# Prologue of a fused attention and mixture-of-experts kernel: the weights loaded on ScalarE's DMA queue beside x, and the order of the first image's statistics, the fold and the memsets rewritten

## The chip, the cores and the metric

The kernel runs as one program on one core of one Trainium2 chip. The metric is the device time in microseconds of that core, the median of several executions. A trace of one profiled execution gives the rows shown below; its engines are TensorE (PE, its weight loads PEld), VectorE (DVE), ScalarE (ACT), GpSimd (POOL) and SyncE (SP). SP, ACT and POOL can also issue DMAs, each on a queue of its own (q1 is SP's, q10 is ACT's, q0 is GpSimd's); all the queues use the same 16 DMA engines.

## The reference, cut to what is computed

```python
# x: (4, 256, 64, 64) float32
x = x + conv_attn(group_norm(x), Wq, bq, Wk, bk, Wv, bv, Wo, bo)
#   conv_attn: instance norm, then for each pixel softmax over its 3x3 neighbours of (q . k) / 16,
#   the weighted sum of v, times Wo, plus bo
t = to_tokens(x)                                     # (4, 4096, 256)
t = t + windowed_gate(layer_norm(t), Wp, bp, Wg)     # sums over a window of 64 tokens
t = t + moe(layer_norm(t), router_w, w1, b1, w2, b2) # 8 experts, top 2
x = from_tokens(t)
```

group_norm and the instance norm need the mean and the variance of all 4096 pixels of an image for each channel, so no pixel of an image can be normalized before all of that image has been read.

## The kernel before, in words

The order of the work is written out by hand. Each engine has its own instruction stream, with explicit semaphores. `enter` and `leave` make a barrier between parts: a part starts when all five engines have left the one before. The parts are a prologue, a token loop (attention, gate, routing) over 32 blocks of 8 image rows (512 tokens, 8 blocks for each of 4 images), a loop over expert tiles, and an output loop. The change touches the prologue and the first lines of the token loop.

The prologue does these things:

- **Weights.** 12 DMAs: the four 256x256 matrices `wq_s`, `wk_s`, `wv_s`, `wo_s` (256 KB each, moved as 256 rows of 1 KB), `wp_s` and `rw_s`, the four biases `bq_s` to `bo_s` (256 single elements of 4 bytes each), `bp_s` and `wg_s`. All raise the semaphore `w_in`, and PE, ACT and DVE all wait for the twelve together (`w_in` at 16 * 12).
- **x of the first image.** Eight DMAs of 512 KB (256 rows of 2 KB each) into the ring `xs` of XR = 8 slots, one semaphore `x_seen` for each slot; then `load_rows(0)`, the first block again with its halo rows into `raw` (3 DMAs). As slots come free (`x_done`), four blocks of the second image follow (EARLY = 4), and then `load_rows(1)` and `load_rows(2)`.
- **Statistics on DVE.** Two `bn_stats` a block (L531) for 12 blocks; after the eighth, `block_means` (L303, L306) aggregates the first image. Then come the group sums: PE multiplies by a block-diagonal matrix (`group_product`, L310), DVE subtracts and squares (`group_spread`, L316 to L320), PE multiplies again, `group_variance` (L325), POOL takes a power of -0.5 (`group_root`, L330), `channel_variance` (L334 to L338), a second power, and `image_scales` (L342, L344).
- **The fold.** PE multiplies Wq by Wk and Wv by Wo, with the bias products (L477, 44 matmuls), ACT copies the results out of PSUM (L499 to L504) and rounds them into the high halves of `wqk2` and `wvo2` (L507), and POOL subtracts to get the low halves (L464), which raises `folded` to 3.
- DVE waits for `folded` at 3, adds `q_const` into `edge` (L541) and raises `prepared`, for which every engine waits on entering the token loop. There DVE's memsets and small copies (L1213 to L1221) raise `cleared` to 5, for which PE, ACT and POOL wait.

The first block of the token loop is normalized by ACT (`normed`, L1024) and POOL (L1578), rounded by ACT (`band`, L1034), and split by DVE (`band_lower`, L1390). PE's first matmul (L758) waits for that. DVE's stream has the statistics of a block of the second image (`x_seen_blocks`, L1411) before `band_lower`; that block, in `xs1`, is loaded by SP as the first thing after `prepared`.

Of the kernel before, what the change touches and what calls it, by code (L numbers as in the profile page):

```python
# [88 lines left out]
def hybrid(nc, x, wqT, wkT, wvT, wo, bq, bk, bv, bo, wpT, bp, wg, rwT, w1, b1, w2, b2, out):  # L89
# [6 lines left out]
    ACT = mybir.ActivationFunctionType  # L96
    AX = mybir.AxisListType

    P = 128
# [29 lines left out]
    with ctx:  # L129
# [118 lines left out]
        def pb(name, shape, dt=f32):  # L248
            return prep.enter_context(nc.sbuf_tensor(name, shape, dt))
# [14 lines left out]
        bo_s = pb("bo_s", [P, CC, 1])  # L264
        bqb = pb("bqb", [P, CC, P])
        XR = 8
        xs = pb("xs", [P, XR, CC, BT])

        w_in = sem("w_in")
        x_in = [sem(f"x_in{i}") for i in range(XROWS)]  # L270
        w_experts = sem("w_experts")
# [83 lines left out]
        def prologue_sync(eng):  # L355
            for dst, src in ((wq_s, wqT), (wk_s, wkT), (wv_s, wvT), (wo_s, wo), (wp_s, wpT), (rw_s, rwT)):
                eng.dma_start(dst[:, :, :], src.rearrange("(c p) n -> p c n", p=P)).then_inc(w_in, 16)
            for dst, src in ((bq_s, bq), (bk_s, bk), (bv_s, bv), (bo_s, bo)):
                eng.dma_start(dst[:, :, :], src.unsqueeze(2)).then_inc(w_in, 16)
            eng.dma_start(bp_s[:, :], bp).then_inc(w_in, 16)  # L360
            eng.dma_start(wg_s[:, :], wg).then_inc(w_in, 16)

            for i in range(XR):
                eng.dma_start(xs[:, i, :, :], xv[:, :, i // IB, i % IB * BT:(i % IB + 1) * BT])\
                   .then_inc(x_seen[i], 16)
            load_rows(eng, 0)
            for i in range(EARLY):
                eng.wait_ge(x_done[i], 1)
                eng.dma_start(xs[:, i, :, :], xv[:, :, 1, i * BT:(i + 1) * BT]).then_inc(x_seen[i], 16)
            for blk in range(1, XROWS):  # L370
                load_rows(eng, blk)
            leave(eng, 0)

        def prologue_gpsimd(eng):
# [85 lines left out]
            eng.wait_ge(pool_const, done)  # L460

            eng.wait_ge(folded, 2)
            for two, whole in ((wqk2, wqk), (wvo2, wvo)):
                last = eng.tensor_tensor(two[:, 1, :, :], whole[:, :, :], two[:, 0, :, :].bitcast(f32),  # L464
                                         ALU.subtract)
            last.then_inc(folded, 1)
            for n in range(2):
                group_root(eng, 0, n)
            leave(eng, 0)

        def prologue_tensor(eng):
            eng.wait_ge(w_in, 16 * 12)
            eng.wait_ge(dve_const, 1)

            def product(bank, cols, lhs, rhs):
                for d in range(CC):
                    last = eng.matmul(bank[:, cols], lhs(d), rhs(d), start=(d == 0), stop=(d == CC - 1))  # L477
                return last
            for c in range(CC):
                cs = slice(c * P, c * P + P)  # L480
                product(m_bank[c], slice(0, C), lambda d: wq_s[:, d, cs], lambda d: wk_s[:, d, :])
                product(m_bank[c], slice(C, C + 1), lambda d: wk_s[:, d, cs], lambda d: bq_s[:, d, :])
                product(m_bank[c], slice(C + 1, C + 2), lambda d: wq_s[:, d, cs], lambda d: bk_s[:, d, :])
                product(m_bank[2 + c], slice(0, C), lambda d: wv_s[:, d, cs], lambda d: wo_s[:, d, :])
                product(m_bank[2 + c], slice(C, C + 1), lambda d: wo_s[:, d, cs], lambda d: bv_s[:, d, :])
            product(s_bank[0], slice(0, 1), lambda d: bqb[:, d, :], lambda d: bk_s[:, d, :]).then_inc(fold, 1)

            eng.wait_ge(pool_const, 23)
            for n in range(2):
                group_product(eng, 0, n, s_bank[1]).then_inc(g_sum, 1)  # L490
            leave(eng, 0)

        def prologue_scalar(eng):
            eng.wait_ge(w_in, 16 * 12)
            eng.wait_ge(kept, 1)
            eng.wait_ge(fold, 1)

            for c in range(CC):
                eng.activation(wqk[:, c, :], m_bank[c][:, 0:C], ACT.Copy, scale=-SCALE)  # L499
                eng.activation(r_bias[:, c, :], m_bank[c][:, C:C + 1], ACT.Copy, scale=-SCALE)  # L500
                eng.activation(wvo[:, c, C:C + 1], m_bank[c][:, C + 1:C + 2], ACT.Copy, scale=-SCALE)
                eng.activation(wvo[:, c, 0:C], m_bank[2 + c][:, 0:C], ACT.Copy)
                eng.activation(o_bias[:, c, :], m_bank[2 + c][:, C:C + 1], ACT.Identity, bias=bo_s[:, c, :])
            eng.activation(q_const[:, :], s_bank[0][:, 0:1], ACT.Copy, scale=-SCALE).then_inc(folded, 1)  # L504
            eng.wait_ge(folded, 1)
            for two, whole in ((wqk2, wqk), (wvo2, wvo)):
                last = eng.activation(two[:, 0, :, :], whole[:, :, :], ACT.Copy)  # L507
            last.then_inc(folded, 1)
            leave(eng, 0)

        def prologue_vector(eng):
            for c in range(CC):
                last = eng.memset(wvo[:, c, C + 1:C + 2], 0.0)
            last.then_inc(kept, 1)
            eng.wait_ge(w_in, 16 * 12)
            eng.tensor_copy(bqb[:, :, :], bq_s[:, :, :].broadcast_to([P, CC, P])).then_inc(dve_const, 1)

            eng.wait_ge(pool_const, 23)
# [7 lines left out]
            eng.tensor_scalar(base[:, 0, :], base0[:, 0, :], float(CAP), None, ALU.mult)  # L526

            for i in range(XR + EARLY):
                eng.wait_ge(x_seen[i % XR], i // XR * 16 + 16)
                for c in range(CC):  # L530
                    last = eng.bn_stats(stats[:, c, i, :], xs[:, i % XR, c, :])  # L531
                last.then_inc(x_done[i % XR], 1)
                if i == XR - 1:
                    eng.wait_ge(x_done[i], 1)
                    block_means(eng, 0)
            group_spread(eng, 0, s_bank[1])
            group_variance(eng, 0, s_bank[1])
            channel_variance(eng, 0)
            image_scales(eng, 0)
            eng.wait_ge(folded, 3)  # L540
# [198 lines left out]
        def token_loop_tensor(eng):  # L739
            enter(eng, 0)  # L740
            eng.wait_ge(prepared, 1)
            eng.wait_ge(cleared, 5)

# [211 lines left out]
        def token_loop_scalar(eng):  # L955
            enter(eng, 0)
            eng.wait_ge(prepared, 1)
            eng.wait_ge(cleared, 5)

# [250 lines left out]
        def token_loop_vector(eng):  # L1210
            enter(eng, 0)
            eng.wait_ge(prepared, 1)
            eng.memset(xn1[:, :, :], 0.0).then_inc(cleared, 1)  # L1213
            eng.memset(tail_id[:, :, :, :], 0.0).then_inc(zeroed, 1)
            eng.memset(blank[:, :, :], 0.0).then_inc(zeroed, 1)
            eng.wait_ge(cleared, 1)
# [3 lines left out]
            eng.memset(xn1[:, :, C:C + 1], 1.0).then_inc(cleared, 1)  # L1220
            eng.memset(besti[:, :, :].rearrange(flat), 0).then_inc(cleared, 1)  # L1221

# [298 lines left out]
        def token_loop_gpsimd(eng):  # L1521
            enter(eng, 0)
            eng.wait_ge(prepared, 1)
            eng.wait_ge(cleared, 5)
            eng.iota(jvec[:, :], pattern=[[1, NJ]], base=0, channel_multiplier=0,
# [506 lines left out]
```

## Time and profile before

| what | value |
|---|---|
| median of 3 runs | 1447.72 us (1446.48 to 1451.52) |
| profiled execution, its own time | 1442.31 us |
| its span in the trace | 1440.5 us |
| busy share of the span: PE, PEld, DVE, ACT, POOL | 89%, 78%, 78%, 69%, 52% |
| first 40.4 us: until PE's first matmul of the token loop | 2.8% of the span |

The busy shares are means over parts with different limits. The profiled execution lies 5.4 us below the median of the others, so a difference worked out on the trace is to be added to the median and not compared with it directly.

### The profile page before, as it was taken

To read this page: it belongs to the slowest core of one execution; us is meant where nothing else is said; L and a number is where in the kernel's file an instruction comes from. 1 tells how busy PE (TensorE), PEld (TensorE's weight loads), DVE (VectorE), ACT (ScalarE), POOL (GpSimd) and SP (SyncE) were. 2 spreads that over 40 slices of the span, in tenths; PEclk is the share of its full clock that TensorE was granted. 3 is DMA by queue.
4 is the path that set the end of the run, shared out by engine and by line. 5 is a ranking of instruction groups with operands and counts; after the bars stand their busy time and mean duration, and the time that the engine had idled before them with its cause. 6 is when DMAs were issued, how large, how long until landed. Compare 5 with 4: busy or idle time off the path is not lost. (4 is left out here: it accounts for less than half of the span.)

```text
span 1440.5 us, 28874 instructions
## 1 busy us (share of the span) xinstructions
PE 1285.4 (89%) x8512; PEld 1130.3 (78%) x8512; DVE 1127.6 (78%) x3903; ACT 987.1 (69%) x2090; POOL 746.9 (52%) x963
## 2 busy tenths in 40 slices
PE   3799999999999999999999589999999999993434
PEld 3688888888888888888887478899999999982334
DVE  5478888888888777878786778899999999983323
ACT  1677777777777777777775468888888888871223
POOL 2115656566656566566655465566566656662000
PEclk9999999999999999999999679999999999996555
DMA  8622535363542122222111189988888888856999
GB/s 273 216 83 80 149 86 148 88 156 89 147 117 91 58 83 64 82 69 86 50 42 57 36 277 326 300 270 270 277 271 270 273 263 275 279 194 273 416 400 350
DMA packets 148216, 264.00 MB, mean 183 GB/s; under 512 B 52576, under 2 KB 74720, under 8 KB 143840
## 3 DMA queue, kind: packets, MB, share of 16 engines
q1 hardware_dynamic: 113440, 173.78, 38.6%
q0 software_dynamic: 25920, 71.60, 14.0%
q10 hardware_dynamic: 8704, 16.78, 3.0%
q8 instruction: 73, 1.20, 0.4%
q14 instruction: 79, 0.65, 0.2%
HBM read 128.39 MB, written 100.68 MB: 159 GB/s over the span
## 5 line engine op out<-in xcount | busy, mean ns | idle before, releaser
L1716 POOL DMA_INDIRECT answers<-yy,dest_i x284 | 276.7, 974 | 176.7 <-DVE yy L1837 99.7
L1558 POOL DMA_INDIRECT sent<-tn,slot_s x256 | 275.5, 1076 | 146.7 <-issue 79.2
L1768 PE MATMUL s_bank<-band,hh 128*128 x568 | 163.2, 287 | 0.6 <-DVE yy L1872 0.6
L1768 PE MATMUL s_bank<-w_s,hh 128*128 x568 | 157.2, 277 | 0.0
L1768 PE MATMUL s_bank<-band,hl 128*128 x568 | 157.0, 276 | 0.0
L1802 ACT ACTIVATE hid<-m_bank,b1s 128x512 f32<-128x512 f32 x142 | 97.7, 688 | 78.3 <-PE m_bank L1751 50.3
L1822 ACT ACTIVATE zz<-xin 128x256 f32<-128x256 f32 x284 | 147.5, 602 | 0.0
L758 PE MATMUL m_bank<-wvo,band 128*128 128x258 f32 x792 | 132.7, 304 | 13.3 <-DVE band L1390 10.9
L1535 POOL TENSOR_TENSOR rs<-ve,halves 128x4 f32<-128x4 f32 x64 | 64.9, 1019 | 153.7 <-DVE ve L1252 153.7
L790 PE MATMUL o_bank<-vv,at 128*128 128x256 f32 x512 | 138.7, 393 | 1.3 <-DVE tt L1300 0.8
L758 PEld LDWEIGHTS m_bank<-wvo,band 128*128 128x128 f32 x792 | 107.1, 192 | 29.4 <-issue 27.7
L1938 PE MATMUL m_bank<-ident,tot 128*128 128x128 f32 x256 | 54.6, 391 | 80.7 <-ACT fin L1952 58.6
L1837 DVE SCALAR_TENSOR_TENSOR yy<-yy,pick,zz 128x256 f32<-128x256 f32 x284 | 118.7, 480 | 7.4
L758 PE MATMUL s_bank<-band,rT 128*128 128x256 f32 x768 | 123.1, 296 | 0.0
L1751 PE MATMUL m_bank<-xh,w1hs 128*128 128x512 f32 x284 | 112.5, 396 | 4.5 <-DMA b2s<-in_b 4.5
L1938 PEld LDWEIGHTS m_bank<-ident,tot 128*128 128x128 f32 x256 | 46.1, 207 | 89.1 <-issue 66.6
L1751 PE MATMUL m_bank<-xh,w1ls 128*128 128x512 f32 x284 | 112.4, 396 | 0.0
L1751 PE MATMUL m_bank<-xl,w1hs 128*128 128x512 f32 x284 | 112.1, 395 | 0.0
L1926 DVE TENSOR_TENSOR tot<-got 128x1024 f32<-128x1024 f32 x32 | 39.1, 1225 | 92.6 <-PE m_bank L1938 64.9
L1952 ACT ACTIVATE fin<-m_bank 128x512 f32<-128x512 f32 x64 | 34.9, 595 | 107.6 <-DMA out_x<-fin 77.1
L1768 PEld LDWEIGHTS s_bank<-band,hh 128*128 128x128 f32 x568 | 106.8, 188 | 0.9 <-issue 0.8
L1768 PEld LDWEIGHTS s_bank<-w_s,hh 128*128 128x128 f32 x568 | 106.9, 188 | 0.1
(238 smaller groups left out, 3658.9 us busy)
## 6 DMA issues: line engine op xcount, KB each, us to landing
xin<-sent SPq DMA_DIRECT2D x71, 524.0 KB, 4.7
got<-answers SPq DMA_DIRECT2D x32, 1024.0 KB, 9.7
w1hs<-rT SPq DMA_DIRECT2D x71, 256.0 KB
w1ls<-w_s SPq DMA_DIRECT2D x71, 256.0 KB
xs<-in_x SPq DMA_DIRECT2D x32, 512.0 KB, 5.0
raw<-in_x SPq DMA_DIRECT2D x32, 512.0 KB
out_x<-fin ACTq DMA_DIRECT2D x32, 512.0 KB, 10.0
b2s<-in_b SPq DMA_DIRECT2D x71, 128.0 KB
```

The lines of the kernel that those rows point to most:

```text
L758: last = eng.matmul(dst, lhs(i, c), rhs(j, c), start=(n == 0), stop=(n == len(passes) - 1))
L790: last = eng.matmul(o_bank[:, 0:C], at[:, k % 2, j, :], vv[:, value_slot(it.block("B"), k + j), 0:C], start=(j == 0), stop=(j == 1))
L1535: eng.tensor_tensor(rs[:, n, :], ve[:, n, :], halves[:, 0, 0:KT], ALU.pow).then_inc(root.sem, 1)
L1558: eng.indirect_dma_start(sent, bass.IndirectOffsetOnAxis(slot_s[:, par, j, k:k + 1], 0), tn[:, par, k, :], None).then_inc(scattered[par], 16)
L1716: eng.indirect_dma_start(answers, bass.IndirectOffsetOnAxis(dest_i[:, at_ % RING, k:k + 1], 0), yy[:, slot, k, :], None).then_inc(rows_out ...
L1751: last = eng.matmul(h_bank[f][:, :], w[:, at_ % WS, c, fs], xx[:, par, c, :], start=(n == 0), stop=(n == 3 * CC - 1))
L1768: last = eng.matmul(y_bank[half][:, k * C:(k + 1) * C], hx[:, par, f, ts], rhs, start=(n == 0), stop=(n == 3 * CC - 1))
L1802: eng.activation(hid[:, f, :], h_bank[f][:, :], ACT.Gelu, bias=b1s[:, at_ % WS, f:f + 1])\
L1822: last = eng.activation(zz[:, at_ % WS, k, :], row[:, 0:C], ACT.Identity, bias=row[:, C + 5:C + 6], scale=row[:, C + 4:C + 5])
L1837: last = eng.scalar_tensor_tensor(row, row, pick[:, at_ % RING, k:k + 1], zz[:, at_ % WS, k, :], ALU.mult, ALU.add)
L1926: eng.tensor_tensor(tot[:, it.parity("K"), :, :], got[:, blk % GOT, :, 0, :], got[:, blk % GOT, :, 1, :], ALU.add).then_inc(tot_ready.sem, 1)
L1938: last = eng.transpose(turned_bank(it, c)[:, k * P:(k + 1) * P], tot[:, it.parity("K"), k, c * P:(c + 1) * P], ident[:, :])
```

## The change

The twelve weight DMAs move from SP's queue to ACT's, each matrix followed by its bias; SP starts with x. The eight DMAs that the fold needs raise a semaphore of their own, `w_fold`; the other four raise `w_in`, for which only PE waits, ahead of the group sums. ACT runs a one-element activation (`warm`) ahead of the fold and takes the fold's results in two halves. DVE does three memsets at the head, moves its constants (L519 to L526) behind the first image's `block_means`, and does the scales of the first image in between the blocks of the second. POOL does the two `group_root` before the fold's subtractions. In the token loop a memset of 1032 columns shrinks to 4.

```diff
@@ prologue_sync
-            for dst, src in ((wq_s, wqT), (wk_s, wkT), (wv_s, wvT), (wo_s, wo), (wp_s, wpT), (rw_s, rwT)):
-                eng.dma_start(dst[:, :, :], src.rearrange("(c p) n -> p c n", p=P)).then_inc(w_in, 16)
-            for dst, src in ((bq_s, bq), (bk_s, bk), (bv_s, bv), (bo_s, bo)):
-                eng.dma_start(dst[:, :, :], src.unsqueeze(2)).then_inc(w_in, 16)
-            eng.dma_start(bp_s[:, :], bp).then_inc(w_in, 16)
-            eng.dma_start(wg_s[:, :], wg).then_inc(w_in, 16)
-
             for i in range(XR):
                 eng.dma_start(xs[:, i, :, :], xv[:, :, i // IB, i % IB * BT:(i % IB + 1) * BT])\
                    .then_inc(x_seen[i], 16)
@@ prologue_gpsimd
+            for n in range(2):
+                group_root(eng, 0, n)
             eng.wait_ge(folded, 2)
             for two, whole in ((wqk2, wqk), (wvo2, wvo)):
                 last = eng.tensor_tensor(two[:, 1, :, :], whole[:, :, :], two[:, 0, :, :].bitcast(f32),
                                          ALU.subtract)
             last.then_inc(folded, 1)
-            for n in range(2):
-                group_root(eng, 0, n)
@@ prologue_tensor
-            eng.wait_ge(w_in, 16 * 12)
+            eng.wait_ge(w_fold, 16 * 8)
             eng.wait_ge(dve_const, 1)
...
-                product(m_bank[2 + c], slice(C, C + 1), lambda d: wo_s[:, d, cs], lambda d: bv_s[:, d, :])
+                product(m_bank[2 + c], slice(C, C + 1), lambda d: wo_s[:, d, cs], lambda d: bv_s[:, d, :]).then_inc(fold, 1)
...
             eng.wait_ge(pool_const, 23)
+            eng.wait_ge(w_in, 16 * 4)
@@ prologue_scalar
-            eng.wait_ge(w_in, 16 * 12)
+            def matrix(dst, src, landed):
+                eng.dma_start(dst[:, :, :], src.rearrange("(c p) n -> p c n", p=P)).then_inc(landed, 16)
+
+            for (dst, src), (bias, given) in (((wq_s, wqT), (bq_s, bq)), ((wk_s, wkT), (bk_s, bk)), ((wv_s, wvT), (bv_s, bv)),
+                                              ((wo_s, wo), (bo_s, bo))):
+                matrix(dst, src, w_fold)
+                eng.dma_start(bias[:, :, :], given.unsqueeze(2)).then_inc(w_fold, 16)
+            matrix(rw_s, rwT, w_in)
+            matrix(wp_s, wpT, w_in)
+            eng.dma_start(bp_s[:, :], bp).then_inc(w_in, 16)
+            eng.dma_start(wg_s[:, :], wg).then_inc(w_in, 16)
             eng.wait_ge(kept, 1)
-            eng.wait_ge(fold, 1)
+            eng.activation(warm[:, :], wvo[:, 0, C + 1:C + 2], ACT.Copy)
+            eng.wait_ge(w_fold, 16 * 8)
 
             for c in range(CC):
+                eng.wait_ge(fold, c + 1)
...
+            eng.wait_ge(fold, CC + 1)
@@ prologue_vector
-            eng.wait_ge(w_in, 16 * 12)
+            eng.memset(tail_id[:, :, :, :], 0.0).then_inc(zeroed, 1)
+            eng.memset(blank[:, :, :], 0.0).then_inc(zeroed, 1)
+            eng.memset(besti[:, :, :].rearrange(flat), 0).then_inc(zeroed, 1)
+            eng.wait_ge(w_fold, 16 * 8)
             eng.tensor_copy(bqb[:, :, :], bq_s[:, :, :].broadcast_to([P, CC, P])).then_inc(dve_const, 1)
+
+            def seen(i, c):
+                if c == 0:
+                    eng.wait_ge(x_seen[i % XR], i // XR * 16 + 16)
+                last = eng.bn_stats(stats[:, c, i, :], xs[:, i % XR, c, :])
+                if c == CC - 1:
+                    last.then_inc(x_done[i % XR], 1)
+
+            for i in range(XR):
+                for c in range(CC):
+                    seen(i, c)
+            eng.wait_ge(x_done[XR - 1], 1)
+            block_means(eng, 0)
 
             eng.wait_ge(pool_const, 23)
...
+            group_spread(eng, 0, s_bank[1])
+            seen(XR, 0)
+            group_variance(eng, 0, s_bank[1])
+            seen(XR, 1)
+            channel_variance(eng, 0)
+            seen(XR + 1, 0)
+            image_scales(eng, 0)
+            seen(XR + 1, 1)
+            for i in range(XR + 2, XR + EARLY):
                 for c in range(CC):
-                    last = eng.bn_stats(stats[:, c, i, :], xs[:, i % XR, c, :])
-                last.then_inc(x_done[i % XR], 1)
...
@@ token_loop_vector
-            eng.memset(xn1[:, :, :], 0.0).then_inc(cleared, 1)
-            eng.memset(tail_id[:, :, :, :], 0.0).then_inc(zeroed, 1)
-            eng.memset(blank[:, :, :], 0.0).then_inc(zeroed, 1)
+            eng.memset(xn1[:, :, C + 1:C + 2], 0.0).then_inc(cleared, 1)
...
-            eng.memset(besti[:, :, :].rearrange(flat), 0).then_inc(cleared, 1)
```

**The weights' DMAs.** On SP, at the start of the program, the weights stood ahead of x before (three more matrices like the first row stand above these rows, and `in_...` is the tensor in HBM):

```order
L357 DMA wo_s<-in_wo 128x2x256
L357 DMA wp_s<-in_wpT 128x2x128
L357 DMA rw_s<-in_rwT 128x2x8
L359 DMA bq_s<-in_bq 128x2
L359 DMA bk_s<-in_bk 128x2
L359 DMA bv_s<-in_bv 128x2
L359 DMA bo_s<-in_bo 128x2
L360 DMA bp_s<-in_bp 128x1
L361 DMA wg_s<-in_wg 128x1
L364 DMA xs<-in_x 128x2x512 x8
```

On ACT, the start of the changed program:

```order
L491 DMA wq_s<-in_wqT 128x2x256
L496 DMA bq_s<-in_bq 128x2
L491 DMA wk_s<-in_wkT 128x2x256
L496 DMA bk_s<-in_bk 128x2
L491 DMA wv_s<-in_wvT 128x2x256
L496 DMA bv_s<-in_bv 128x2
L491 DMA wo_s<-in_wo 128x2x256
L496 DMA bo_s<-in_bo 128x2
L491 DMA rw_s<-in_rwT 128x2x8
L491 DMA wp_s<-in_wpT 128x2x128
L499 DMA bp_s<-in_bp 128x1
L502 ACT_TABLE_LOAD
```

All twelve left SP, where the eight DMAs of x now stand first; on ACT each bias stands behind its matrix.

**The first image's scales.** On DVE before, from the end of `block_means` to the end of the prologue (`g` stands for g1, g2 and g3):

```order
L306 COPY g<-mv 128x2
L531 BN_STATS stats<-xs 128x6 x8
L316 TENSOR_TENSOR g<-g,s_bank 128x2
L318 TENSOR_TENSOR g<-g 128x2
L320 TENSOR_TENSOR g<-g,mv 128x2
L325 TENSOR_SCALAR g<-s_bank 128x2
L334 TENSOR_TENSOR g<-g 128x2
L336 TENSOR_TENSOR g<-g,mv 128x2
L338 TENSOR_SCALAR g<-g 128x2
L342 TENSOR_TENSOR s_all<-g 128x2
L344 SCALAR_TENSOR_TENSOR b_all<-g,s_all 128x2
L541 TENSOR_SCALAR edge<-edge,q_const 128x1
```

On DVE in the changed program, from the second instruction of `group_spread` on:

```order
L320 TENSOR_TENSOR g<-g 128x2
L322 TENSOR_TENSOR g<-g,mv 128x2
L533 BN_STATS stats<-xs 128x6
L327 TENSOR_SCALAR g<-s_bank 128x2
L533 BN_STATS stats<-xs 128x6
L336 TENSOR_TENSOR g<-g 128x2
L338 TENSOR_TENSOR g<-g,mv 128x2
L340 TENSOR_SCALAR g<-g 128x2
L533 BN_STATS stats<-xs 128x6
L344 TENSOR_TENSOR s_all<-g 128x2
L346 SCALAR_TENSOR_TENSOR b_all<-g,s_all 128x2
L533 BN_STATS stats<-xs 128x6 x5
```

The eight `bn_stats` of the second image stood ahead of the chain; now three stand inside it and five behind it.

**The powers and the fold on POOL.** Before, at the end of the prologue and the start of the token loop:

```order
L464 TENSOR_TENSOR wqk<-wqk 128x512
L464 TENSOR_TENSOR wvo<-wvo 128x516
L330 TENSOR_TENSOR g<-g,halves 128x2 x2
L1525 IOTA jvec 128x71
L1529 IOTA tail_id 128x60
```

The same place in the changed program:

```order
L332 TENSOR_TENSOR g<-g,halves 128x2 x2
L461 TENSOR_TENSOR wqk<-wqk 128x512
L461 TENSOR_TENSOR wvo<-wvo 128x516
L1545 IOTA jvec 128x71
L1549 IOTA tail_id 128x60
```

The two powers moved ahead of the two subtractions.

## Rows read from the trace of the kernel before

**Rows 1.** The page: busy tenths of PE in 40 slices.

```profile
PE   3799999999999999999999589999999999993434
```

**Rows 2.** Timeline of SP's issues: start, us, engine, line.

```profile
0.80 0.45 SPq L357 DMA_DIRECT2D wq_s<-in_wqT  x1
...
6.26 0.43 SPq L361 DMA_DIRECT2D wg_s<-in_wg  x1
...
33.39 5.78 SPq L707 DMA_DIRECT2D xs<-in_x  x3
```

**Rows 3.** Timeline, the fold on PE and DVE beside it.

```profile
8.33 0.29 DVE L516 COPY bqb<-bq_s 128x256 f32<-128x256 f32 x1 [7.37 <-DMA wg_s<-in_wg]
...
8.77 2.04 PE L477 MATMUL m_bank<-wk_s,wq_s 128*128 128x256 f32 x4 [8.77 <-DVE bqb L516]
...
13.91 8.05 DVE L531 BATCH_NORM_STATS2 stats<-xs 128x6 f32<-128x512 f32 x12 [0.67 <-DMA xs<-in_x]
...
20.71 0.99 PE L477 MATMUL s_bank<-bk_s,bqb 128*128 128x1 f32 x4
```

**Rows 4.** Timeline, the first image's scales.

```profile
22.63 0.17 DVE L306 COPY g<-mv 128x2 f32<-128x2 f32 x1
...
29.27 0.14 DVE L316 TENSOR_TENSOR g<-g,s_bank 128x2 f32<-128x2 f32 x1
...
29.86 0.59 PE L310 MATMUL s_bank<-g,group 128*128 128x2 f32 x2 [6.36 <-DVE g L320]
30.49 0.16 DVE L325 TENSOR_SCALAR g<-s_bank 128x2 f32<-128x2 f32 x1 [0.68 <-PE s_bank L310]
...
31.48 0.16 DVE L334 TENSOR_TENSOR g<-g 128x2 f32<-128x2 f32 x1 [0.84 <-POOL g L330]
...
32.12 0.70 POOL L330 TENSOR_TENSOR g<-g,halves 128x2 f32<-128x2 f32 x1 [0.67 <-DVE g L338]
...
33.13 0.27 DVE L541 TENSOR_SCALAR edge<-edge,q_const 128x1 f32<-128x1 f32 x1
```

**Rows 5.** Timeline, the fold's copies on ACT and POOL.

```profile
21.81 1.28 ACT L499 ACT_TABLE_LOAD   x1 [21.81 <-PE s_bank L477]
...
25.50 0.62 ACT L507 ACTIVATE wvo<-wvo 128x516 fp32r<-128x516 f32 x1
26.26 1.26 POOL L464 TENSOR_TENSOR wqk<-wqk 128x512 fp32r<-128x512 f32 x1 [17.34 <-ACT wvo L507]
```

**Rows 6.** Timeline, the start of the token loop.

```profile
33.78 0.92 DVE L1213 MEMSET xn<- 128x1032 f32 x1 [0.39 <-DVEq L350]
...
35.78 1.52 ACT L1024 ACTIVATE normed<-raw,b_all,s_all 128x512 f32<-128x512 f32 x2 [9.67 <-issue]
...
37.33 1.27 ACT L1034 ACTIVATE band<-normed 128x1280 fp32r<-128x1280 f32 x1
37.49 1.29 DVE L1411 BATCH_NORM_STATS2 stats<-xs 128x6 f32<-128x512 f32 x2 [1.88 <-DMA xs<-in_x]
...
38.70 1.54 DVE L1390 TENSOR_TENSOR band<-normed,band 128x640 fp32r<-128x640 f32 x2
...
40.39 1.63 PE L758 MATMUL m_bank<-wvo,band 128*128 128x258 f32 x6 [9.94 <-DVE band L1390]
```

**Rows 7.** Windows: length, busy of each engine, PEclk, DMA share, GB/s last.

```profile
0.00:2.00 2.00, 0.00 (x0) 0.00 (x0) 0.09 (x2) 0.00 (x0) 1.11 (x10) 1.00 0.06 5
2.00:4.00 2.00, 0.00 (x0) 0.00 (x0) 0.00 (x0) 0.00 (x0) 1.50 (x7) 1.00 0.94 292
...
10.00:15.00 5.00, 5.00 (x19) 4.46 (x19) 3.67 (x6) 0.00 (x0) 0.00 (x0) 1.00 1.04 394
```

**Rows 8.** DMA queues, 6 to 8 us: packets, MB, share of 16 engines.

```profile
q1 hardware_dynamic: 887, 0.09, 41.0%
```

**Rows 9.** DMA queues, 1370 to 1376 us, in the output loop.

```profile
q1 hardware_dynamic: 275, 1.99, 79.8%
q10 hardware_dynamic: 280, 0.54, 23.2%
```

More of the change, by code:

```diff
@@ L265, in hybrid @@
         bqb = pb("bqb", [P, CC, P])
+        warm = pb("warm", [P, 1])
         XR = 8
@@ L269, in hybrid @@
         w_in = sem("w_in")
+        w_fold = sem("w_fold")
         x_in = [sem(f"x_in{i}") for i in range(XROWS)]
@@ L526, in prologue_vector @@
             eng.tensor_scalar(base[:, 0, :], base0[:, 0, :], float(CAP), None, ALU.mult)
-            for i in range(XR + EARLY):
-                eng.wait_ge(x_seen[i % XR], i // XR * 16 + 16)
-                for c in range(CC):
-                    last = eng.bn_stats(stats[:, c, i, :], xs[:, i % XR, c, :])
-                last.then_inc(x_done[i % XR], 1)
[L533 to L539, printed above, removed]
+            group_spread(eng, 0, s_bank[1])
[7 more added lines that the diff above has]
+            for i in range(XR + 2, XR + EARLY):
+                for c in range(CC):
+                    seen(i, c)
             eng.wait_ge(folded, 3)
@@ L741, in token_loop_tensor @@
             eng.wait_ge(prepared, 1)
-            eng.wait_ge(cleared, 5)
+            eng.wait_ge(cleared, 4)
             def begin(it, job):
@@ L957, in token_loop_scalar @@
             eng.wait_ge(prepared, 1)
-            eng.wait_ge(cleared, 5)
+            eng.wait_ge(cleared, 4)
             def take(it, job, out_, in_=None, func=ACT.Copy, **k):
@@ L1523, in token_loop_gpsimd @@
             eng.wait_ge(prepared, 1)
-            eng.wait_ge(cleared, 5)
+            eng.wait_ge(cleared, 4)
             eng.iota(jvec[:, :], pattern=[[1, NJ]], base=0, channel_multiplier=0,
```

## The prediction

> **What bounds the kernel now.** I read the page's slices first. PE is at nine tenths or more from the third slice to the 36th, except in two slices in the middle, where one part gives way to the next [rows 1]. So what stands ahead of the token loop is a serial head: a microsecond more or less in it should reach the end nearly whole, since no part behind it runs to a clock of its own. The change works only in that head, which is why the rest of the trace matters little here.
>
> The timeline of the first 41 us gives the head as three stretches. Call W the moment when DVE sees the weights.
>
> - Until W = 8.33, PE and DVE do nothing of note: the last weight, issued at 6.26, is what both wait for [rows 2, 3].
> - From W on, PE folds until 21.70 (20.71 + 0.99), which is W + 13.4, while DVE takes statistics as fast as x lands [rows 3]. The chain of the scales then ends with `edge` at 33.13, and SP issues the first load of the token loop at 33.39: `prepared` is at W + 25.1 [rows 2, 4].
> - From 33.39 to PE's first matmul at 40.39 it is 7.0 us [rows 2, 6].
>
> What matters in this reading is that both engines hang on W, and that the chain from `group_spread` (29.27) to 33.13 waits for nothing but DVE's queue: the group sum was due long before, `mv` being copied at 22.63, but the blocks of the second image stand in front [rows 4].
>
> **The part after W, which gets shorter.** In the changed order DVE goes from W into 16 statistics at 0.671 each (8.05 / 12) [rows 3], 10.7 us, and has the means about 0.9 later, at W + 12.0. Seven constants follow, each a copy of the size of `bqb` (0.29) or smaller, so at most 2.0 us in the 2.1 until the group sum is there. PE is the later one: it ends the fold at W + 13.4, does the group product, and its result reaches DVE 0.63 later, as from 29.86 to 30.49 [rows 4]: `group_spread` starts at W + 14.1. The chain itself took 3.86 us (29.27 to 33.13) [rows 4]. The three statistics put inside it lie in its waits (about 29.8 to 30.49, 30.65 to 31.48, 32.1 to 32.82): 0.67 fits each time but for 0.05 us. Five remain behind it, 3.36 us, and 0.26 from `edge` to SP's issue. Sum: 14.1 + 3.86 + 0.05 + 3.36 + 0.26 = W + 21.6. That is 3.4 us less than W + 25.1.
>
> POOL's swap costs nothing: ACT ends its rounding at about W + 15 now that the 1.28 us table load is ahead of the fold and half of the copies lie beside PE (before: 26.12) [rows 5]. The powers end at W + 17.6, and the two subtractions of 2.5 us follow (1.26 and as much again, [rows 5]), so `folded` is 3 at W + 20.2, 1.2 us before DVE asks. Without that cover each microsecond would count. The table load and the halves are hidden likewise. The three early memsets lie before W.
>
> The shorter memset of the token loop looks like 0.9 us off the path (33.78 to 34.70), and with the moved ones I estimate 1.4 of the 2.0 us until ACT starts at 35.78 [rows 6]. I cost it at nothing. DVE's statistics of the block in `xs1` stand in front of `band_lower`, and they wait until 37.49 for a load that SP issued at 33.39; they end at 38.78, after ACT's `band` at 38.60 [rows 2, 6]. With ACT 1.4 us earlier the load still decides: 4.1 + 1.3 + 1.6 = 7.0 us from `prepared` to PE, as before. The bound from the other side is 1.4 us gained.
>
> **W itself, which gets later.** Before, the weights had the DMA engines to themselves. Now x is on SP's queue from the same moment. The trace of before has no two queues competing in the prologue, but the output loop has: SP loads 8 KB packets, ACT stores 2 KB packets, both with more queued than is moved. From 1370 to 1376 us the queues moved 275 and 280 packets, 1.99 and 0.54 MB [rows 9]. The turn goes one packet to each queue, whatever its size.
>
> Now count packets. The fold needs 4 x 256 rows of 1 KB and 4 x 256 single elements of a bias: 2048 packets. Against each stands one row of x of 2 KB, and SP has 8 x 256 = 2048 of these queued, and `raw` behind them, before it waits for anything. The small biases, 4 KB in all, are the costly half: each element lets a 2 KB row of x pass. So the eight weight DMAs land when all eight blocks of x have gone too:
>
> - x, 4.19 MB at 394 GB/s [rows 7]: 10.6 us;
> - matrices, 1.05 MB at 292 GB/s [rows 7]: 3.6 us;
> - biases: 887 mostly small packets took 41% of 2 us [rows 8], 14.8 ns of one engine each, so 1024 of them over 16 engines 0.95 us.
>
> 15.2 us, from the first packet at 2.0 (the share is 0.06 before, 0.94 after) [rows 7], and some 0.8 from the last packet to the wait that sees it: of the 2.07 from the last weight's issue at 6.26 to 8.33, 1.2 is what the first issue at 0.80 took to its first packet [rows 2, 3, 7]. An estimate: W = 18.0 instead of 8.33.
>
> The bounds: with equal bytes for both queues W would be 10.7 (below); with the weights first, 7.3; with small packets or pairs dearer than alone, 21. I take 18.0, because the six microseconds of [rows 9] are two queues of this core, both backlogged, and nothing in them favours either.
>
> DVE cannot use x while it waits: `bqb` stands ahead of the statistics and needs `w_fold`. That is the second half of the cost, for x's first block will lie there from about 5.5 us (2.0, 16 pairs of packets on each engine, and the landing).
>
> **Sum.** `prepared` moves from 33.4 to 18.0 + 21.6 = 39.6: +6.2 us. PE's first matmul of the loop comes at 46.6. On the profiled execution that is 1442.3 + 6.2 = 1448.5, on the median 1447.7 + 6.2 = 1453.9. What a measurement of this kernel can tell from no change is 0.3%, 4.3 us; W = 11.8 would be no change, above 16.1 it can be told.
>
> The Trainium skill speaks against this edit too. "DMA: Bandwidth & Descriptors", section "Issuing engines are not separate DMA queues", says that issuing from several engines saves only the sequencer's time and that the transfers interleave on the same 16 engines. The trace agrees: both queues share one stretch in [rows 9].
>
> **Rivals.**
>
> *Larger turns.* If several small packets went in one turn, up to 4 KB, four rows of weights would face two of x, and a bias's 16 elements on an engine one turn. Then 40 rows of x pass on each engine, 1.31 MB or 3.3 us, and W = 2.0 + 3.3 + 3.6 + 0.95 + 0.8 = 10.7. `prepared` is at 32.3: -1.1 us, 1446.6. For it speaks that the packets of [rows 9] are too large and too few in size to show a grouping of 4-byte ones; against it, that 2 KB packets went one by one there and not two by two. The same page of the Trainium skill, section "SWDGE vs HWDGE vs iDMA", describes for GpSimd's path a packet of preferably up to 4096 bytes as the unit after which an engine turns to another queue; no row of before shows that for ACT's.
>
> *The weights win, and it ends faster.* If ACT's queue is served ahead of x, for instance since SP's descriptors for 2 KB rows come slower than the engines ask, the fold's data take 2.0 + 3.6 + 0.95 + 0.8: W = 7.3. `prepared` at 28.9, -4.5 us, 1443.2; the point from which this is faster by over 0.3% is W = 7.5. Four of the twelve DMAs no longer count for the wait, which speaks for some gain; equal turns in [rows 9] against it.
>
> *The delay does not reach the end.* W is late as forecast, but part of the 6.2 us is given back, say 3 or more, as the clock granted to PE or the meeting of transfers in the loops changes. 1450 or so. PE's dense slices [rows 1] speak against it.
>
> **How the numbers follow.** One packet a turn, W between 16 and 21, time 1452 to 1457: 0.58. Larger turns: 0.23. Weights first: 0.09. Delay given back: 0.10. Over 4.3 us slower is most of the first, 0.51; faster is the third with a little of the second, 0.12; the rest within. The range leaves out a tenth on each side: from 1444.5, where the faster cases begin, to 1458.5, W = 21 with a microsecond or so of spread. The likeliest case alone is 1451.5 to 1457.5.
>
> **What would show it.** In the trace after: DVE's `bqb` at about 18 (the whole forecast hangs on it); equal counts of packets on q1 and q10 from 2 to 17 us; PE's fold 13.4 long from there; statistics without a wait for x, 16 in a row; `group_spread` at W + 14; `folded` before DVE asks; `prepared` at W + 21.6; from there 7.0 to PE, with the wait for `xs1` still in front of `band_lower`. It is wrong if `bqb` comes before 12, or if PE's first loop matmul moves and the end does not.

## The result and the profile after

The changed kernel takes 1452.19 us (median of 20 runs, 1447.24 to 1457.92), the kernel before in the same sets 1448.75 us (20 runs, 1442.49 to 1453.54). The ratio is 1.0025, 95% interval 1.0013 to 1.0037: 3.4 us slower by the medians, 3.6 by the ratio (0.0025 of 1449). That is a loss, since the interval does not reach 1 (it stands for 1.9 to 5.4 us), and it is smaller than the 4.3 us that the prediction set as what can be told. 1453.9 was forecast. Ratios here and below leave out runs over 1.5% above the fastest of the same kernel, while medians take in all runs.

The timeline of the changed kernel, rows that answer to [rows 2 to 6] (start, us, engine, line, operation):

```profile
0.81 4.71 SPq L359 DMA_DIRECT2D xs<-in_x  x8
0.81 0.49 ACTq L491 DMA_DIRECT2D wq_s<-in_wqT  x1
...
5.05 0.55 ACTq L496 DMA_DIRECT2D bo_s<-in_bo  x1
...
15.46 0.29 DVE L528 COPY bqb<-bq_s 128x256 f32<-128x256 f32 x1 [13.78 <-DMA bo_s<-in_bo]
15.67 9.58 DVE L533 BATCH_NORM_STATS2 stats<-xs 128x6 f32<-128x512 f32 x16
...
15.90 2.05 PE L472 MATMUL m_bank<-wk_s,wq_s 128*128 128x256 f32 x4 [15.90 <-DVE bqb L528]
...
27.84 0.99 PE L472 MATMUL s_bank<-bk_s,bqb 128*128 128x1 f32 x4
...
29.29 0.16 DVE L318 TENSOR_TENSOR g<-g,s_bank 128x2 f32<-128x2 f32 x1 [2.45 <-PE s_bank L312]
...
32.90 1.26 POOL L461 TENSOR_TENSOR wqk<-wqk 128x512 fp32r<-128x512 f32 x1
32.96 1.21 DVE L344 TENSOR_TENSOR s_all<-g 128x2 f32<-128x2 f32 x1 [0.21 <-POOL g L332]
34.12 1.27 POOL L461 TENSOR_TENSOR wvo<-wvo 128x516 fp32r<-128x516 f32 x1
34.21 1.20 DVE L346 SCALAR_TENSOR_TENSOR b_all<-g,s_all 128x2 f32<-128x2 f32 x1
35.33 3.05 DVE L533 BATCH_NORM_STATS2 stats<-xs 128x6 f32<-128x512 f32 x5
35.59 5.47 SPq L730 DMA_DIRECT2D xs<-in_x  x3
38.30 0.25 DVE L564 TENSOR_SCALAR edge<-edge,q_const 128x1 f32<-128x1 f32 x1
...
39.15 1.52 ACT L1047 ACTIVATE normed<-raw,b_all,s_all 128x512 f32<-128x512 f32 x2 [8.93 <-issue]
...
39.38 1.29 DVE L1431 BATCH_NORM_STATS2 stats<-xs 128x6 f32<-128x512 f32 x2 [0.40 <-DMA xs<-in_x]
...
42.00 1.56 DVE L1410 TENSOR_TENSOR band<-normed,band 128x640 fp32r<-128x640 f32 x2 [1.33 <-ACT band L1057]
...
43.71 1.63 PE L781 MATMUL m_bank<-wvo,band 128*128 128x258 f32 x6 [13.23 <-DVE band L1410]
```

Read it from the fold's weights. The last of them, a bias of 1 KB, was issued at 5.05 and landed 10.4 us later: `bqb` comes at 15.46 instead of 8.33 [rows 3], so W is 7.1 us late. From there the way to the loop is shorter than before: DVE's 16 statistics run without a wait (9.58 us), the group sum is used at W + 13.8 instead of 20.9 [rows 4], and PE's first loop matmul stands at W + 28.25 instead of W + 32.06 [rows 3, 6]. 7.13 lost and 3.81 won give 43.71 instead of 40.39: +3.32 us. The end moved by 3.4 to 3.6 us, which agrees within the interval.

The DMA queues of the changed kernel from 3 to 15 us (packets, MB, share of 16 engines; q1 carries x, q10 the weights):

```profile
q1 hardware_dynamic: 1733, 3.35, 76.7%
q10 hardware_dynamic: 1681, 1.03, 28.8%
```

As many packets of the one as of the other, though x moved three times the bytes.

### The profile page after: what moved, and what is told of

The parts are those of the page before. It is cut to its first block and busy times, and to the rows that moved or that the text cites. A ratio compares the mean times of both kernels' runs of the same rounds, so it can differ in the third digit from the quotient of the medians.

```text
span 1454.7 us, 28875 instructions
## 1 busy us (share of the span) xinstructions
PE 1291.1 (89%) x8512; PEld 1131.6 (78%) x8512; DVE 1128.3 (78%) x3903; ACT 988.1 (68%) x2091; POOL 752.1 (52%) x963
## 5 line engine op out<-in xcount | busy, mean ns | idle before, releaser
L1736 POOL DMA_INDIRECT answers<-yy,dest_i x284 | 279.7, 985 | 174.4 <-DVE yy L1857 100.5
L813 PE MATMUL o_bank<-vv,at 128*128 128x256 f32 x512 | 143.9, 405 | 1.4 <-DVE tt L1320 0.8
```

Source lines behind the costliest of these rows:

```text
L813: last = eng.matmul(o_bank[:, 0:C], at[:, k % 2, j, :], vv[:, value_slot(it.block("B"), k + j), 0:C], start=(j == 0), stop=(j == 1))
L1736: eng.indirect_dma_start(answers, bass.IndirectOffsetOnAxis(dest_i[:, at_ % RING, k:k + 1], 0), yy[:, slot, k, :], None).then_inc(rows_out ...
```

## The experiments

The kernels were timed in three sets, on three chips. In the first set the kernel before took 1448.7 us, in the other two 1561.9 and 1609.8 (medians); ratios and differences of the device time are always within a set. The head of the program differs little between them: with the weights' DMAs as changed and unsplit, the fold's weights were there between 15.46 and 16.12 us in all three. So positions in the timelines are compared across sets, best as distances from W. The kernel before was traced in the first set alone.

### The weights back on SP, ahead of x

```diff
@@ prologue_sync
+            for (dst, src), (bias, given) in (((wq_s, wqT), (bq_s, bq)), ((wk_s, wkT), (bk_s, bk)), ((wv_s, wvT), (bv_s, bv)),
+                                              ((wo_s, wo), (bo_s, bo))):
+                matrix(dst, src, w_fold)
+                eng.dma_start(bias[:, :, :], given.unsqueeze(2)).then_inc(w_fold, 16)
...
             for i in range(XR):
@@ prologue_scalar
-            for (dst, src), (bias, given) in (((wq_s, wqT), (bq_s, bq)), ((wk_s, wkT), (bk_s, bk)), ((wv_s, wvT), (bv_s, bv)),
-                                              ((wo_s, wo), (bo_s, bo))):
...
```

The four DMAs that raise `w_in` move along.

Expected:

> The changed kernel with its twelve weight DMAs back on SP's queue ahead of x, all else as changed. Theory (the head decides, and the weights' landing is what got late): bqb comes at about 7 us instead of 15.5 (1.05 MB at 292 GB/s, 512 small packets, 2.0 ahead and 0.8 behind), the statistics are again as fast as x lands, and PE's first matmul of the token loop comes at about 38 us: 2.4 us ahead of the kernel before, 5.7 ahead of the change. Device time about 1446.5 where before is 1448.8. Rival (the other edits, or the loops, carry the loss): it stays at or above the kernel before.

Measured: 1445.74 us (12 runs) beside 1448.68, ratio 0.9991 (0.9972 to 1.0009). The timeline:

```profile
7.50 0.56 DVE L528 COPY bqb<-bq_s 128x256 f32<-128x256 f32 x1 [5.82 <-DMA bo_s<-in_bo]
...
10.60 10.78 DVE L533 BATCH_NORM_STATS2 stats<-xs 128x6 f32<-128x512 f32 x16 [2.54 <-DMA xs<-in_x]
...
37.39 1.63 PE L781 MATMUL m_bank<-wvo,band 128*128 128x258 f32 x6 [13.23 <-DVE band L1410]
```

PE starts the loop 6.3 us ahead of the change and 3.0 ahead of before, and DVE now waits for x instead of for the weights. The place of the weights is the loss: nothing else was edited, and this ratio's interval lies wholly below the change's (1.0013 to 1.0037). Whether this kernel is faster than the one before the interval leaves open (2.9 us by the medians, 1.3 by the ratio).

### Only the queue

```diff
@@ prologue_sync
-            for dst, src in ((wq_s, wqT), (wk_s, wkT), (wv_s, wvT), (wo_s, wo), (wp_s, wpT), (rw_s, rwT)):
-                eng.dma_start(dst[:, :, :], src.rearrange("(c p) n -> p c n", p=P)).then_inc(w_in, 16)
...
@@ prologue_scalar
+            for dst, src in ((wq_s, wqT), (wk_s, wkT), (wv_s, wvT), (wo_s, wo), (wp_s, wpT), (rw_s, rwT)):
+                eng.dma_start(dst[:, :, :], src.rearrange("(c p) n -> p c n", p=P)).then_inc(w_in, 16)
...
```

This is an edit of the kernel before: all twelve DMAs in their old order, each still raising `w_in`.

Expected:

> The kernel before with its twelve weight DMAs moved to ACT's queue in their old order, and nothing else. Theory: all twelve land at about 20 us, beside x; from there 22.2 us to SP's first load of the loop and 7.0 to PE: first loop matmul at about 49.4 us instead of 40.4, device time about 9 us over before (0.6%). The other edits of the change must then be worth some 5.5 us. Rival (the queue costs nothing, the order on DVE does): within 1.5 us of before.

Measured: 1460.55 us (6 runs) beside 1448.68, ratio 1.0090 (1.0061 to 1.0118).

```profile
20.02 0.29 DVE L515 COPY bqb<-bq_s 128x256 f32<-128x256 f32 x1 [19.06 <-DMA wg_s<-in_wg]
...
41.16 0.16 DVE L334 TENSOR_TENSOR g<-g 128x2 f32<-128x2 f32 x1 [3.72 <-POOL g L330]
...
50.03 1.63 PE L757 MATMUL m_bank<-wvo,band 128*128 128x258 f32 x6 [12.78 <-DVE band L1389]
```

The queue alone costs 9.6 us in the head (50.03 - 40.39), inside the interval of 8.8 to 17.1 us at the end, though nearer to its lower bound than its centre of 13.0. The other edits, taken together, are thus worth 6.3 us of it (9.6 - 3.3), and 4.6 of these are W itself (20.02 against 15.46): eight DMAs to wait for instead of twelve, and another order.

The second row shows what POOL's swap takes away. With the subtractions still ahead of the powers, DVE waits 3.72 us for the first power, since POOL is at the subtractions from 37.96 to 40.4. In the kernel before they had been over by 28.8, ahead of the chain.

### The same bytes in twice the packets

```diff
@@ prologue_scalar, matrix()
-                eng.dma_start(dst[:, :, :], src.rearrange("(c p) n -> p c n", p=P)).then_inc(landed, 16)
+                for h in range(halves_of):
+                    cols = slice(h * C // 2, (h + 1) * C // 2) if halves_of == 2 else slice(None)
+                    eng.dma_start(dst[:, :, cols], src[:, cols].rearrange("(c p) n -> p c n", p=P)).then_inc(landed, 16)
```

Expected:

> The changed kernel with each of the four matrices moved as two DMAs of half rows: the same bytes, 2048 packets of 512 B instead of 1024 of 1 KB. Theory (one packet a turn): 2560 packets must go instead of 1536, and as many of SP's go with them, so bqb moves from 15.5 to about 19.6 us and PE's first loop matmul by about 4 us. Rival (bytes or larger turns decide): bqb stays within 0.7 us of 15.5.

`halves_of` is 2 for the four matrices of the fold. Measured: one time, 1454.30 us. The timeline, and the DMA queues from 3 to 19 us:

```profile
20.50 0.29 DVE L531 COPY bqb<-bq_s 128x256 f32<-128x256 f32 x1 [18.82 <-DMA bo_s<-in_bo]
...
26.90 1.85 PE L472 MATMUL m_bank<-wk_s,wq_s 128*128 128x256 f32 x4
...
29.40 1.11 PE L472 MATMUL m_bank<-wo_s,wv_s 128*128 128x256 f32 x4
...
46.21 1.63 PE L784 MATMUL m_bank<-wvo,band 128*128 128x258 f32 x6 [13.23 <-DVE band L1413]
```

```profile
q1 hardware_dynamic: 2809, 4.63, 81.3%
q10 hardware_dynamic: 2911, 1.06, 26.6%
```

W moved by 5.0 us (4.1 expected, 0 by bytes): it is the count of packets. The counts are near equal again. The 0.9 us beyond the expectation is not explained; from 19 to 20.5 us SP's queue was nearly empty (84 packets against 639), so the last of the weights no longer met x. PE's first loop matmul moved by only 2.5 us, which the theory did not have: four matmuls of the fold took 2.04 to 2.06 us up to 26.9, 1.85 in the group that begins there, and 1.11 from 29.4 on. The expectation's 4 us for it is a miss.

### Matmuls on PE while it waits

```diff
@@ prologue_tensor
+            eng.wait_ge(pool_const, 5)
+            for n in range(56):
+                eng.matmul(s_bank[1][:, 256:384], ones[:, :], ones[:, :], start=True, stop=True)
             eng.wait_ge(w_fold, 16 * 8)
```

Expected:

> The changed kernel with 56 matmuls of 128x128 ones on PE while it waits for the weights (their result is not used). Theory (the fold's matmuls run at half their later speed because PE comes from idling: in the run with half rows their duration fell from 0.51 to 0.28 us midway): the fold takes about 7 us instead of 12.9, the group sum waits for DVE instead, group_spread starts at about 26.9 instead of 29.3, and PE's first loop matmul comes 2.4 us earlier, at about 41.3. Rival (the speed belongs to something else, DMA traffic for one): the fold takes 12.9.

Measured: one time, 1549.37 us, in the set where before took 1561.92 (one run, from which no difference is read).

```profile
1.90 15.56 PE L469 MATMUL s_bank<-ones 128*128 128x128 f32 x112 [1.90 <-POOL ones L383]
15.79 0.29 DVE L531 COPY bqb<-bq_s 128x256 f32<-128x256 f32 x1 [14.12 <-DMA bo_s<-in_bo]
...
17.29 1.03 PE L475 MATMUL m_bank<-wk_s,wq_s 128*128 128x256 f32 x4
...
23.34 0.58 PE L475 MATMUL s_bank<-bk_s,bqb 128*128 128x1 f32 x4
...
41.58 1.63 PE L784 MATMUL m_bank<-wvo,band 128*128 128x258 f32 x6 [13.22 <-DVE band L1413]
```

Each of the 56 stands as two rows in the trace. The fold takes 6.6 us (17.29 to 23.92) instead of 12.9, though it starts 1.5 us behind W, when the 56 are through, and PE comes to the loop at W + 25.8, 2.5 us sooner. So the fold ran at half this speed in the kernel before and in the changed one. In none of the eleven traces without these matmuls did it start at the higher speed. In two it reached it midway (the one with half rows and the second run of the change), in nine never, and what decides between these the runs do not show. DMA traffic does not: the two stretches shown at the end of this document had 352 and 346 GB/s.

### POOL's subtractions behind the scales

```diff
@@ prologue_gpsimd
             for n in range(2):
                 group_root(eng, 0, n)
+            eng.wait_ge(scaled_images, 1)
             eng.wait_ge(folded, 2)
```

Expected:

> The changed kernel with one more wait: POOL starts the fold's two subtractions only when image_scales is done. Theory (DVE's two small operations of image_scales took 1.21 and 1.20 us instead of 0.16 because POOL's subtractions ran beside them): they take 0.16 to 0.17 again, the last statistics end 2.1 us earlier, folded is at 3 about 0.6 us later, and PE's first loop matmul comes at about 42.8 us instead of 43.7. Rival (they were slow for the value they waited for, not for POOL): they stay at 1.2 us. The device time can't tell it.

Measured: one time, 1444.27 us.

```profile
15.90 0.29 DVE L529 COPY bqb<-bq_s 128x256 f32<-128x256 f32 x1 [14.22 <-DMA bo_s<-in_bo]
...
33.40 0.16 DVE L344 TENSOR_TENSOR s_all<-g 128x2 f32<-128x2 f32 x1 [0.22 <-POOL g L332]
33.59 0.17 DVE L346 SCALAR_TENSOR_TENSOR b_all<-g,s_all 128x2 f32<-128x2 f32 x1
...
43.20 1.63 PE L782 MATMUL m_bank<-wvo,band 128*128 128x258 f32 x6 [12.28 <-DVE band L1411]
```

The two operations are back at 0.16 and 0.17 us, so it was POOL's instruction beside each that held them for its whole length. PE's first loop matmul stands at W + 27.3, 0.95 us sooner. The rest of the 2.1 us is lost at the load of `xs1`, for which DVE waits 2.98 us in this run: SP issues it at 36.53, W + 20.6 instead of W + 20.1, since `folded` comes later.

### The statistics not behind the weights

```diff
@@ prologue_vector
-            eng.wait_ge(w_fold, 16 * 8)
-            eng.tensor_copy(bqb[:, :, :], bq_s[:, :, :].broadcast_to([P, CC, P])).then_inc(dve_const, 1)
...
-            for i in range(XR):
+            for i in range(XR + EARLY):
+                if i == 6:
+                    eng.wait_ge(w_fold, 16 * 8)
+                    eng.tensor_copy(bqb[:, :, :], bq_s[:, :, :].broadcast_to([P, CC, P])).then_inc(dve_const, 1)
                 for c in range(CC):
                     seen(i, c)
+                if i == XR - 1:
+                    eng.wait_ge(x_done[XR - 1], 1)
+                    block_means(eng, 0)
...
             group_spread(eng, 0, s_bank[1])
-            seen(XR, 0)
             group_variance(eng, 0, s_bank[1])
-            seen(XR, 1)
...
```

PE waits for `dve_const` only ahead of its last product, and no `seen` is left between the steps of the scales.

Expected:

> The changed kernel with DVE's statistics no longer behind the weights: bqb is copied ahead of the seventh block, PE waits for it only before its last product, and all twelve blocks stand ahead of the scales. The DMAs stay as changed. Theory (DVE's wait for the fold's weights costs only what it leaves behind the group sum, PE's fold is the later one): the group sum still starts at about 29 us, but no statistics stand behind the scales, which POOL's subtractions again draw out to about 35.4; edge at about 35.7 and PE's first loop matmul at about 41.1 us instead of 43.7. Rival (PE alone decides): 43.7 stays.

Measured: 1562.82 us (10 runs) beside 1561.92, ratio 1.0031 (0.9993 to 1.0069).

```profile
15.85 2.07 PE L471 MATMUL m_bank<-wk_s,wq_s 128*128 128x256 f32 x4 [15.85 <-DMA bo_s<-in_bo]
...
35.41 0.27 DVE L559 TENSOR_SCALAR edge<-edge,q_const 128x1 f32<-128x1 f32 x1
...
39.41 1.29 DVE L1426 BATCH_NORM_STATS2 stats<-xs 128x6 f32<-128x512 f32 x2 [3.20 <-DMA xs<-in_x]
...
42.31 1.63 PE L776 MATMUL m_bank<-wvo,band 128*128 128x258 f32 x6 [11.85 <-DVE band L1405]
```

`edge` came where it was expected (35.7), 2.9 us sooner than in the changed kernel, but PE gained only 1.4 where 2.6 was expected: the load of `xs1` lands at the same time (39.41 against 39.38) and is last again, as before the change [rows 6]. The statistics in the way cost less than the path behind them hides. At the end nothing can be told (the interval stands for -1.1 to 10.8 us).

### The wide memset

```diff
@@ token_loop_vector
-            eng.memset(xn1[:, :, C + 1:C + 2], 0.0).then_inc(cleared, 1)
+            eng.memset(xn1[:, :, :], 0.0).then_inc(cleared, 1)
```

Expected:

> The changed kernel with the memset of 1032 columns back at the head of the token loop. Theory (in the changed kernel the path at the loop's start runs over DVE's memsets and ACT, since the load of xs1 is now issued before edge is done): PE's first loop matmul moves by nearly the whole 0.9 us, from 43.7 to about 44.5. Rival, as in the prediction (the load hides the memset): 43.7 stays.

Measured: one time, 1559.80 us.

```profile
39.29 0.92 DVE L1236 MEMSET xn<- 128x1032 f32 x1 [0.16 <-issue]
...
45.35 1.63 PE L781 MATMUL m_bank<-wvo,band 128*128 128x258 f32 x6 [14.29 <-DVE band L1410]
```

`bqb` came at 16.03 and PE's first loop matmul at 45.35, W + 29.3, which is 1.1 us later, counted from W, than in the changed kernel. In the changed kernel the memset is on the path; in the kernel before it was behind the load of `xs1`.

### All the places at once, and the change again

The kernel for this has the weights on SP and POOL's wait as above, `bqb` copied ahead of the sixth block, with PE waiting for it only ahead of its last product (the statistics of the second image stay inside and behind the scales), and one edit more:

```diff
@@ token_loop_vector, body()
-                x_seen_blocks(it)
+                if it.off > -2:
+                    x_seen_blocks(it)
...
                 if n:
                     band_lower(it)
+                if it.off == -2:
+                    x_seen_blocks(it)
```

Expected:

> The changed kernel with the weights on SP ahead of x, the subtractions behind the scales, bqb copied ahead of the sixth block, and in the loop's first step the statistics of xs1 behind band_lower. Theory (each of these costs was found where it stands, and they add up): the scales are done at about 27, edge at 30.3, ACT starts the first block at 31.1, and PE's first loop matmul comes at about 35.7 us, 4.7 ahead of the kernel before; device time about 1444 where before is 1448.7. Rival (what the head saves is lost in the loop, for its first steps wait for loads): less than half of 4.7 arrives.

Measured: 1552.82 us (12 runs) beside 1561.92, ratio 0.9950 (0.9913 to 0.9987).

```profile
30.25 0.26 DVE L566 TENSOR_SCALAR edge<-edge,q_const 128x1 f32<-128x1 f32 x1
...
31.10 1.52 ACT L1049 ACTIVATE normed<-raw,b_all,s_all 128x512 f32<-128x512 f32 x2 [9.39 <-DVE xn L1243]
...
33.96 1.56 DVE L1412 TENSOR_TENSOR band<-normed,band 128x640 fp32r<-128x640 f32 x2 [3.03 <-ACT band L1059]
35.44 1.28 DVE L1433 BATCH_NORM_STATS2 stats<-xs 128x6 f32<-128x512 f32 x2
...
35.67 1.63 PE L783 MATMUL m_bank<-wvo,band 128*128 128x258 f32 x6 [11.15 <-DVE band L1412]
```

The head is 4.7 us shorter than before the change, step by step as expected. The same kernel a second time, and the changed kernel beside it:

> The kernel of e9_first_block_ahead once more, since the set before ran where the kernel before took 1562 instead of 1449 us. Theory (what the head saves arrives at the end): 4.7 us under the kernel before of this set, ratio about 0.9967. Rival (the loops swallow or add as much): outside 0.9967 by more than 0.0015.

> The changed kernel as it is, beside the other of this set on one chip. Theory (the head's 3.3 us are the whole loss): ratio to the kernel before about 1.0023, and bqb between 15 and 16.5 us. Rival: a loss in the loops adds to it, and the ratio lies above 1.004.

Measured: 1600.06 us (12 runs) beside 1609.78 for the first, ratio 0.9955 (0.9928 to 0.9981); 1610.95 us (12 runs) for the change, ratio 1.0017 (0.9985 to 1.0049). Neither contradicts the head: on 1610 us the 4.7 saved and the 3.3 lost would be 0.9971 and 1.0021 (the expectations had 0.9967 and 1.0023, worked out on 1449). The combined kernel beats the one before in two sets and the change in the one where both ran, where their intervals do not touch. By their centres the two ratios save 7.8 and 7.2 us, more than the 4.7 of the head; the intervals hold both, so whether the loops give anything is open. For the change this second set tells little: its interval holds 1, and in the profiled execution the fold sped up midway (its last product took 0.58 us), so PE's first loop matmul came at 41.66, only 1.3 us later than in the kernel before.

## Why the prediction was right, and where its steps were off

**The queue (right in kind, one term too large).** The step that carried the forecast was "one packet a turn". What it says of the shares holds: equal counts on both queues in the changed kernel (1733 and 1681), and 1024 more packets of weights move W by 5.0 us at equal bytes. Whether the engines take one packet a turn or the same few of each queue, counts don't show, and the sum does not need it. The rival of larger turns for smaller packets would have given 10.7 for W, that of the weights first 7.3; both fell. The mis-sized term is "4 x 256 single elements of a bias". A bias is 128 packets of 8 bytes. The trace of before already had it; its queue from 0 to 50 us:

```profile
q1 hardware_dynamic: 9024, 11.03, 66.8%
```

36 DMAs were issued by then. Their rows are 15 x 256 for x, 9 x 256 for `raw`, 6 x 256 for the six matrices and 2 x 128 for `bp_s` and `wg_s`, 7936 in all. With 16 closing packets for each DMA, 576, that leaves 9024 - 7936 - 576 = 512 for the four biases, 128 each. The fold's packets are 1536 and not 2048, so 1536 rows of x pass: 3.15 MB or 8.0 us, and 0.5 for the biases; by the prediction's own sum W = 2.0 + 8.0 + 3.6 + 0.5 + 0.8 = 14.9. Measured 15.46. So this term is 3.1 us too large, and 0.6 of it was made up for elsewhere: by 14.7 us, 0.8 ahead of W, SP's queue had moved 3.42 MB and not 3.15. Part of that is its earlier start: by 2.7 us it had moved 59 packets and ACT's queue 5. The kernel section's "256 single elements of 4 bytes each" is wrong in the same way.

**After W (the sum right by luck, its parts wrong both ways).** Forecast W + 21.6 + 7.0 = W + 28.6, measured W + 28.25. That these agree to 0.4 us is luck, for misses of opposite sign cancel: SP issued the load of `xs1` at W + 20.1 instead of 21.6, and from there to PE it took 8.1 us instead of 7.0. Inside it:

- The fold and the group sum came as forecast: `group_spread` at W + 13.8 (14.1).
- "16 statistics at 0.671 each" was too slow. The twelve of [rows 3] ran while x was still landing; the sixteen, with x there, took 9.58 us, not 10.7, and the five behind the scales 3.05, not 3.36. Of the sixteen nothing was gained, since PE was the later one.
- "POOL's swap costs nothing" failed. With the powers first, the two subtractions run from 32.90 to 35.39, over `image_scales`, whose two operations took 1.21 and 1.20 us. Before, the same subtractions lay beside `bn_stats` [rows 5], which they did not slow (a median of 0.68 us each beside them, 0.69 just ahead of them). The prediction asked only who waits for `folded`, and not who computes beside it. It costs 2.1 us on DVE and 0.95 in the end. That does not make the swap a loss: ACT ended its rounding at 30.22 and the first power was asked for at about 30.8, so without the swap the subtractions would have held up the powers, as they did in the run with only the queue. The changed order without the swap was not run.
- "0.26 from `edge` to SP's issue" failed, and made the load earlier. SP issued at 35.59, 0.2 after `folded` was 3, while `edge` ran at 38.30. `prepared` is raised by an instruction of its own behind `edge`; the five statistics and `edge` ahead of it had nothing left to wait for once `folded` was 3, and it was seen before they had run. So the load of `xs1` started 2.7 us ahead of `edge`, and 1.5 us ahead of the forecast W + 21.6.
- "I cost it at nothing" for the memset fell with that. With the load early, ACT's `normed` and `band` became last: DVE waited 0.40 for the load and 1.33 for `band`, and the wide memset costs 1.1 us there.

**Range and chances.** 1452.19 lies in the range and in the likeliest case's 1451.5 to 1457.5, but W, at 15.46, lies just below the 16 to 21 on which that case was built. Some of the closeness in time is luck: the size went from +6.2 to +3.4 us, a miss of 2.8, while the time missed by only 1.7, because the kernel before took 1448.75 us in the comparison and 1447.72 in the three runs that the forecast started from. The miss in size is the biases' term, and it went from over to under what was set as tellable, which 20 runs of each could tell all the same. As far as the interval of 1.9 to 5.4 us shows, the delay of 3.3 in the head reached the end, and 3 us of it were not given back, so that rival fell too. One side remark came true to the tenth: with the statistics free of the weights, x's first block was taken up at 5.55 us (5.5 forecast).

The Trainium skill's "DMA: Bandwidth & Descriptors", "Issuing engines are not separate DMA queues", was borne out: ACT's queue saved the issue time, 6 us of SP's, and paid it back by interleaving, W + 7.1. For the collision its page "SBUF — State Buffer", section "SBUF: two separate sides", says that a DVE operation with two SBUF inputs and a GpSimd operation take a shared port pair one after the other, each for its whole instruction. The trace agrees: 1.21 and 1.20 us beside POOL's 1.26 and 1.27, and 0.16 and 0.17 where POOL was kept away, while `bn_stats` with one input kept its pace.

## What to carry to other kernels

SP's and ACT's queues shared the DMA engines by packets and not by bytes: a transfer that others wait for, in rows shorter than those of its neighbour, gave away three quarters of the bytes (1.03 MB against 3.35), so put it first on one queue, and take its packets from the count of the trace and not from the shape in the code. When an operation is moved behind another, ask also what will now run beside it on other engines: two operations of 0.16 us took 1.2 here. And before calling an edit hidden, recompute the cover with the other edits in place: here the change itself removed what had hidden the memset.

## What the runs showed of the hardware that was not expected

- **PE at half speed in a short stretch.** Four fold matmuls of 128x256 took 2.05 us after PE had idled, and 1.03 to 1.11 us where 15 us of matmuls stood ahead; with half rows and in the second run of the change the step came within the fold, 6 to 7.7 us after its start, and in the other nine traces not within its 12.9. The granted clock shown was 1.00 of full speed (the level of 2.4 GHz) in all of it. This row is the fold of the changed kernel, the next that of the kernel with matmuls ahead (the third number from the end is PEclk, behind it the DMA share and GB/s):

```profile
15.90:28.80 12.90, 12.90 (x45) 11.47 (x45) 10.88 (x26) 1.72 (x10) 0.00 (x0) 1.00 1.07 352
```

```profile
17.30:23.90 6.60, 6.60 (x46) 6.13 (x44) 6.60 (x12) 1.31 (x8) 0.00 (x0) 1.00 1.07 346
```

  So the shown clock did not tell the two speeds apart here; the durations do.
- **A semaphore raised ahead of the operation in front of it.** `prepared` was seen by SP at 35.59, and `edge`, which stands ahead of it on DVE, ran at 38.30. The same shows with half rows (38.09 and 40.81) and with the wide memset (36.16 and 38.87). An increment that must follow an operation belongs on that operation, as `folded` has it.
- **The sets differ by up to 11%.** The same kernel before took 1448.7, 1561.9 and 1609.8 us, each time on another chip. In the slower sets the head was hardly longer, but ACT and DVE had waits that the profile puts down to "remote". All six traces of those sets have them, and none of the six at about 1450 us. The longest of the second run of the change (who waited, for whom, us, times, longest):

```profile
ACT hid L1822 <- remote: 96.0, 21, 6.2
```

  What the remote side is was not found out, and one chip for each set does not separate chip from time.
